# Issuing a step's side tasks between its two score groups in a two-layer attention kernel

## The chip, the cores and the metric

One core of one Trainium2 chip runs the whole kernel. The metric is device time in microseconds; three executions of the kernel before gave 825.37, 826.34 and 826.98 us (median 826.34).

## What is computed

`x` is 8 images of 32 x 32 positions with 128 channels, all float32. Two layers follow each other:

```
layer 0: t   = layernorm(x); q, k, v = t @ w_qkv + b_qkv            (8 heads of 16)
         out = softmax(q k^T / 4) v ;  x = x + out @ w_out + b_out  (1024 queries x 1024 keys per head)
layer 1: tokens = x @ Win + b_in ; t = layernorm(tokens) ; q, k, v = t @ Wq, Wk, Wv
         pk, pv = 4 x 4 means of k and v (64 positions)
         scores of all queries against pk; the 16 positions with the largest maximum are selected
         attention over those 16; tokens += result
         t2 = layernorm(tokens); tokens += gelu(t2 @ Wf1 + bf1) @ Wf2 + bf2
         out = tokens @ Wout + bout
```

## The kernel before

Almost all of the work is the attention of layer 0. For one image it is cut into 32 **steps** (`STEPS`): four pairs of heads (`PAIRS`) times eight blocks of 128 keys (`TILES`). In step s of image n

- TensorE makes the **scores** of both heads for two halves of the queries: `scores(n, s, 0)` and `scores(n, s, 1)` (L611), two matmuls each (L621). They go to the two halves `S[:, 0]` and `S[:, 1]` of one PSUM tensor. The first group waits until the first exponential of the step before has read its half, the second until the second has;
- ScalarE turns each group into probabilities, `exps(n, s, 0)` and `exps(n, s, 1)` (L846, L852): one ACTIVATE over 128 x 1024 each, into one of three buffers `Pr`;
- TensorE makes the **weighted sums** of the values, `weighted(n, s)` (L625, L636), eight matmul records for each step of keys. `sums_behind` (L80) says which are issued in step s. In images 0 and 7, and in the first 13 steps of image 1, it is the step before; everywhere else odd steps have none, and even ones those of the two steps before. Two are left behind step 31;
- VectorE divides a pair's sums (`divide_o`, L1063) once its eight steps are done, and SyncE moves the result into `attnT`.

Everything else is hung into these steps as **tasks**, by fixed tables (`AT_...`, `USUAL`, `ENDING`, L54 to L63): `before_tasks` prepare the next image (normalise and transpose, steps 6 and 10; q in 17 and 19; k in 21 and 23; v in 25 and 29; the bound on the scores in 28 and 30; the token projection in 32 and 37, which are steps 0 and 5 of the image's own attention); `after_tasks` do layer 1 of the image before (projection 3, transposes 12, q 13, pooled keys 15, scores of the selection 18 to 21 (L687), their maximum 22 (L693) and 23, selection 25, attention over the 16 in 27 to 31, and, already in the steps of the image after, the feed-forward part in 33 to 43, which are 1 to 11). So steps 2, 4, 14, 16, 24 and 26 have no TensorE task. Image 7 and what follows it use `ENDING`.

TensorE fills one PSUM bank with a task's result (`A` for `before_tasks`, `BC0` and `BC1` in turn for `after_tasks`), and VectorE or ScalarE empties it; a later task waits until its bank is empty (`a_turn`, `b_turn`) or its input is there (`b_ready` and other waits). Every engine works through its instructions in the order in which the program gives them. ScalarE and VectorE have their own loops over the steps: ScalarE does the two exponentials of a step and then its share of that step's tasks (L920 to L929); VectorE only its tasks, with `divide_o` at the head of steps 8, 16 and 24.

TensorE's loop before is

```
for s in range(STEPS):
    scores(n, s, 0)
    scores(n, s, 1)
    for behind in sums_behind(n, s):
        weighted(n, behind)
    (the tasks of step s)
```

Of the kernel before, what the change touches and what calls it, by code (L numbers as in the profile page):

```python
# [33 lines left out]
TILES = T // P  # L34
# [6 lines left out]
STEPS = PAIRS * TILES  # L41
# [38 lines left out]
def sums_behind(n, s):  # L80

    if n in (0, IMAGES - 1) or (n == 1 and s < LIGHT):
        return (s - 1,) if s > 0 else ()
    return (s - 2, s - 1) if s % 2 == 0 and s > 0 else ()


def xn_steps(n):
# [46 lines left out]
def two_layers(nc, x, ln_scale, ln_bias, w_qkv, b_qkv, w_out, b_out, Win, b_in, Wq, Wk, Wv, g1, be1, g2, be2,  # L134
# [11 lines left out]
    with ExitStack() as ctx:  # L146
# [132 lines left out]
        def wait_for_flag(eng, n):  # L279

            if n == 0:
                eng.wait_ge(first_dve, FIRST_FLAG)
            else:
                eng.wait_ge(a_drained, a_after(n, "flag", 0))
# [254 lines left out]
        def _(pe):  # L539
# [23 lines left out]
            def before_tasks(n, s):  # L563
                if s in xn_steps(n):
                    h = xn_steps(n).index(s)
                    pe.wait_ge(xn_ready, n + 1)
                    a_turn(n, "xn", h)
                    for t in range(4):
                        mm = pe.transpose(A[:, t * P:(t + 1) * P], xn[:, 4 * h + t, :], ident[:, :])
                    mm.then_inc(a_filled, 1)  # L570
                if s in AT_Q + AT_K:
                    c, h = (0, AT_Q.index(s)) if s in AT_Q else (C, AT_K.index(s))
                    a_turn(n, "k" if c else "q", h)
                    pe.matmul(A[:, :], wqkv_s[:, c:c + C], half(xnT, h), start=True, stop=True).then_inc(a_filled, 1)  # L574
                if s in AT_V:
                    a_turn(n, "v", AT_V.index(s))
                    by_token(A, a_filled, [(xnT, wqkv_s[:, 2 * C:3 * C])], AT_V.index(s))
                if s in AT_TOKX:
                    a_turn(n, "tokx", AT_TOKX.index(s))
                    by_token(A, a_filled, [(xhT, win_s[:, :])], AT_TOKX.index(s))  # L580
                if s == AT_BOUND:
                    pe.wait_ge(squares_ready, n)
                    a_turn(n, "bound", 0)
                    sums_of_squares(A, a_filled)
                if s == AT_FLAG:
                    a_turn(n, "flag", 0)
                    pe.transpose(A[0:1, 0:P], peak[:, :], ident[:, :]).then_inc(a_filled, 1)

            def row_maxima(n):

                for j in range(PAIRS):
                    pe.wait_ge(stack_in[j], 32 + 16 * STACK_DMAS * (n + 1))
                if n > 0:
                    pe.wait_ge(probs_ready, 2 * STEPS * n)
                pe.sem_inc(pe_passed, 1)
                with pe.Fori(0, TILES) as t:
                    pe.wait_ge(tile_copied, TILES * n + t + 1)
                    for h in range(HEADS):
                        pe.wait_ge(max_drained, MAX_TILES * n + HEADS * t + h + 1)
                        r = 64 * (h % 2)  # L600
                        for c in range(2):
                            mm = pe.matmul(S[:, h % 2, c * HALF:(c + 1) * HALF], Qt[r:r + MROW, h // 2, :],
                                           Ks[r:r + MROW, h // 2, c * HALF:(c + 1) * HALF], start=True, stop=True)
                        mm.then_inc(max_filled, 1)
                pe.wait_ge(max_drained, 2 + MAX_TILES * (n + 1))
                pe.sem_inc(pe_passed, 1)
                pe.transpose(S[0:MAX_TILES, 0, 0:P], mx[:, :], ident[:, :]).then_inc(max_turned, 1)
                pe.wait_ge(mneg_ready, n + 1)
                pe.wait_ge(mrow_in, 16 * HEADS * (n + 1))

            def scores(n, s, c):  # L611

                j, kb = s // TILES, s % TILES
                before = 2 * STEPS * n + 2 * s + c - 1
                if before > 0:
                    pe.wait_ge(probs_ready, before)
                if kb == 0 and c == 0:
                    pe.wait_ge(stack_in[j], 32 + 16 * STACK_DMAS * (n + 1))
                for a in range(2):
                    head = slice(64 * a, 64 * a + MROW + 1)  # L620
                    mm = pe.matmul(S[:, c, a * HALF:(a + 1) * HALF], Ks[head, j, kb * P:(kb + 1) * P],  # L621
                                   Qs[head, j, c * HALF:(c + 1) * HALF], start=True, stop=True)
                mm.then_inc(scores_ready, 1)

            def weighted(n, s):  # L625

                j, kb = s // TILES, s % TILES
                pe.wait_ge(probs_ready, 2 * STEPS * n + 2 * s + 2)
                if kb == 0:
                    pe.wait_ge(va_ready, PAIRS * n + j + 1)  # L630
                    if n > 0 or j > 0:
                        pe.wait_ge(o_turned, PAIRS * n + j)
                for a in range(2):
                    for c in range(2):
                        r = 32 * (2 * a + c)
                        mm = pe.matmul(O[r:r + 32, :], Va[:, kb, 2 * j + a, :], Pr[:, (STEPS * n + s) % 3, c, a * HALF:(a + 1) * HALF],  # L636
                                       start=(kb == 0), stop=(kb == TILES - 1))
                mm.then_inc(pv_done, 1)
# [161 lines left out]
            def image(n):  # L800

                wait_for_flag(pe, n)
                pe.sem_inc(pe_passed, 1)
                with pe.If(pe.value_load(flag[0:1, 0:1], min_val=0, max_val=HEADS) > 0):
                    row_maxima(n)
                with pe.Else():
                    pe.sem_inc(max_filled, MAX_TILES)
                    pe.sem_inc(max_turned, 1)
                for s in range(STEPS):
                    scores(n, s, 0)  # L810
                    scores(n, s, 1)
                    for behind in sums_behind(n, s):
                        weighted(n, behind)
                    if n > 0:
                        before_tasks(n, STEPS + s)
                    if n + 1 < IMAGES:
                        before_tasks(n + 1, s)
                    if n > 1:
                        after_tasks(n - 2, STEPS + s)
                    if n > 0:  # L820
                        after_tasks(n - 1, s)
                for behind in sums_behind(n, STEPS):
                    weighted(n, behind)

            image(0)

            pe.wait_ge(weights_in, 16 * WEIGHT_DMAS)
            pe.wait_ge(first_dve, FIRST_DVE)
            for n in range(1, IMAGES):
                image(n)  # L830
# [499 lines left out]
```

## Time and profile before

| | |
|---|---|
| median of three executions | 826.34 us |
| the profiled execution | 827.2 us, its span 825.5 us |
| TensorE busy | 778.4 us (94%) |
| ScalarE busy | 604.1 us (73%) |
| VectorE busy | 506.5 us (61%) |
| GpSimd busy | 164.5 us (20%) |
| TensorE clock, mean over the span | 0.983 of full speed |

The times in the rows are microseconds from the start of the span. PE is TensorE, ACT ScalarE, DVE VectorE, POOL GpSimd. Busy time of an engine is the union of its instructions, so that overlapping matmuls count once and a short wait inside a merged group doesn't show as idle. Images 2 to 6 repeat every 92.2 us; image 3 begins at 278.3, image 7 at 647.2.

### The profile page before, as it was taken

Reading aid. Unit: us, or ns where it says so; the run is one execution under the profiler, and the core shown is the slowest. Engines: PE = TensorE matmul, PEld = TensorE weight load, DVE = VectorE, ACT = ScalarE, POOL = GpSimd, SP = SyncE. Lnnn points to the kernel's source line nnn. Section 1 sums busy time; section 2 is a strip of 40 time slices with the busy share of each in tenths; the row PEclk is TensorE's granted clock in tenths of the full one; section 3 lists DMA queues with packets and bytes.
Section 4 is the critical chain, followed back from the end, with each engine's and each line's share of the span. In section 5 each row is a group of like instructions: output and inputs, shape, how many; then the busy total and the mean of one; then the engine's idle time right before and its main releaser. Section 6 shows DMA issues by size and latency. Waiting matters only on the chain.

```text
span 825.5 us, 14363 instructions
## 1 busy us (share of the span) xinstructions
PE 778.4 (94%) x5079; PEld 373.3 (45%) x5079; DVE 506.5 (61%) x1518; ACT 604.1 (73%) x683; POOL 164.5 (20%) x198
## 2 busy tenths in 40 slices
PE   8889899999999999999999999999999989899987
PEld 6322343355534544355534554354534444245555
DVE  6415446777567865777567865777367753367465
ACT  4697789778887788778878788778878677574112
POOL 2620523221241032121141033112011011000100
PEclk9999999999999999999999999999999999699979
DMA  3553343333243252333253253324153232200400
GB/s 73 95 91 70 66 73 76 72 65 59 58 115 53 47 97 56 81 59 64 54 119 53 45 96 71 73 51 72 21 122 55 48 62 54 55 8 7 103 0 26
DMA packets 45308, 52.89 MB, mean 64 GB/s; under 512 B 15920, under 2 KB 33968, under 8 KB 45232
## 3 DMA queue, kind: packets, MB, share of 16 engines
q1 hardware_dynamic: 45232, 51.92, 32.5%
q8 instruction: 42, 0.69, 0.4%
q14 instruction: 34, 0.28, 0.1%
HBM read 5.45 MB, written 4.19 MB: 12 GB/s over the span
## 4 chain that ended last, share of the span: by engine, by line
PE 62%; ACT 15%; issue 6%; DVE 5%; ACTq 0%; DVEq 0%
PE O L636 21%; PE S L621 15%; ACT Pr L852 10%; PE BC L650 6%; PE BC L642 3%; PE BC L687 3%; PE BC L733 2%; PE BC L747 2%; PE BC L669 2%; PE A L650 2%; PE A L574 2%; PE S L836 1%; ACT hT L892 1%; ACT L852 1%; ACT L892 1%
## 5 line engine op out<-in xcount | busy, mean ns | idle before, releaser
L852 ACT ACTIVATE Pr<-S 128x1024 f32<-128x1024 f32 x512 | 491.5, 1029 | 123.5 <-PE S L621 119.8
L636 PE MATMUL O<-Pr,Va 128*32 128x512 f32 x2048 | 256.7, 606 | 1.8 <-DVE OT L1069 1.1
L621 PE MATMUL S<-Qs,Ks 49*128 49x512 f32 x1024 | 217.3, 471 | 24.6 <-ACT Pr L852 22.0
L621 PEld LDWEIGHTS S<-Qs,Ks 49*128 49x128 f32 x1024 | 87.6, 185 | 172.3 <-ACT Pr L852 135.0
L636 PEld LDWEIGHTS O<-Pr,Va 128*32 128x32 f32 x2048 | 50.0, 109 | 104.6 <-issue 96.9
L501 POOL TENSOR_TENSOR q1l<-q1T,q1h 128x1024 fp32r<-128x1024 f32 x8 | 19.1, 2389 | 217.5 <-DVE q1h L1119 217.5
L1143 DVE TENSOR_REDUCE r<-BC 128x1 f32<-128x512 f32 x64 | 41.4, 685 | 32.7 <-PE BC L687 32.5
L1069 DVE STREAM_TRANSPOSE OT<-O 128x512 f32<-128x512 f32 x32 | 22.8, 713 | 52.1 <-PE O L636 51.9
L462 POOL TENSOR_SCALAR xn<-X,ln 128x128 f32<-128x128 f32 x56 | 45.8, 830 | 3.7 <-DVE ln L982 3.7
L493 POOL TENSOR_TENSOR squares<-qh 128x1024 bf16<-128x1024 f32 x7 | 13.3, 1893 | 151.2 <-DVE hot L1165 112.4
L515 POOL TENSOR_TENSOR tokx<-tokx_new,tok_bias 128x1024 f32<-128x1024 f32 x8 | 19.0, 2370 | 120.1 <-DVE tokx_new L988 120.1
L867 ACT ACTIVATE tT<-BC,cols 128x512 f32<-128x512 f32 x32 | 23.4, 778 | 24.1 <-PE BC L642 24.1
L1210 DVE TENSOR_SCALAR hT<-BC,cols 128x512 f32<-128x512 f32 x32 | 24.0, 751 | 26.5 <-PE BC L733 25.0
L484 POOL TENSOR_SCALAR tokx_new<-win_sum,ln 128x128 f32<-128x128 f32 x64 | 37.4, 605 | 1.4 <-POOL tokx L515 1.3
L1215 DVE TENSOR_TENSOR Y<-BC,out_bias 128x512 f32<-128x512 f32 x16 | 11.0, 690 | 42.9 <-PE BC L747 42.9
L473 POOL COPY Va<-v_new 128x256 f32<-128x256 f32 x32 | 11.8, 399 | 112.9 <-PE O L636 95.5
L687 PE MATMUL BC<-Q1s,K1s 96*128 96x512 f32 x64 | 31.0, 561 | 3.1 <-issue 2.4
L733 PE MATMUL BC<-tT,wf_s 128*128 128x512 f32 x64 | 31.7, 616 | 1.1 <-ACT tT L867 0.5
L747 PE MATMUL BC<-w2o,hT 128*128 128x128 f32 x256 | 32.1, 280 | 0.0
L747 PEld LDWEIGHTS BC<-w2o,hT 128*128 128x128 f32 x256 | 29.6, 192 | 4.7 <-issue 4.7
L574 PE MATMUL A<-xnT,wqkv_s 128*128 128x512 f32 x56 | 31.5, 645 | 0.0
L886 ACT ACTIVATE E<-E 128x512 f32<-128x512 f32 x16 | 9.4, 632 | 26.8 <-DVE E L1182 26.7
(189 smaller groups left out, 989.6 us busy)
## 6 DMA issues: line engine op xcount, KB each, us to landing
Qs<-qh SPq DMA_DIRECT2D x128, 64.0 KB, 2.3
Ks<-kh SPq DMA_DIRECT2D x128, 64.0 KB, 2.3
Q1s<-q1h SPq DMA_DIRECT2D x64, 128.0 KB, 2.4
X<-in_x_dram SPq DMA_DIRECT2D x8, 512.0 KB, 4.2
Qs<-ql SPq DMA_DIRECT2D x64, 64.0 KB, 2.4
Ks<-kl SPq DMA_DIRECT2D x64, 64.0 KB, 2.3
attnT<-On SPq DMA_DIRECT2D x128, 32.0 KB, 2.0
Q1s<-q1l SPq DMA_DIRECT2D x32, 128.0 KB, 2.4
```

What stands on the lines that cost most here:

```text
L462: ins = pool.tensor_scalar(xn[:, t, :], X[:, t, :], ln[:, 0, t:t + 1], ln[:, 1, t:t + 1], ALU.subtract, ALU.mult)
L484: ins = pool.tensor_scalar(tokx_new[:, t, :], win_sum[:, :], ln0[n % 2][:, 0, t:t + 1], None, ALU.mult)
L574: pe.matmul(A[:, :], wqkv_s[:, c:c + C], half(xnT, h), start=True, stop=True).then_inc(a_filled, 1)
L621: mm = pe.matmul(S[:, c, a * HALF:(a + 1) * HALF], Ks[head, j, kb * P:(kb + 1) * P], Qs[head, j, c * HALF:(c + 1) * HALF], start=True, sto ...
L636: mm = pe.matmul(O[r:r + 32, :], Va[:, kb, 2 * j + a, :], Pr[:, (STEPS * n + s) % 3, c, a * HALF:(a + 1) * HALF], start=(kb == 0), stop=(k ...
L642: mm = pe.transpose(bank[:, t * P:(t + 1) * P], src[:, 4 * h + t, :], ident[:, :])
L650: mm = pe.matmul(bank[:, t * P:(t + 1) * P], lhs[:, c:c + P], w, start=(i == 0), stop=(i == len(pairs) - 1))
L687: pe.matmul(bank[:, :], K1s[:, j, :, :].rearrange("p a b -> p (a b)"), half(Q1s[0:ROWS1, j, :], h), start=True, stop=True).then_inc(filled, 1)
L733: pe.matmul(bank[:, :], wf1_s[:, f * C:(f + 1) * C], half(tT, h), start=True, stop=True)\
L747: mm = pe.matmul(BC[h][:, t * P:(t + 1) * P], hT[:, f, c:c + P], w2o[:, f, :], start=False, stop=(t == 3 and f == 1))
L852: act.activation(Pr[:, g % 3, c, :], S[:, c, :], ACT.Exp, scale=SCALE).then_inc(probs_ready, 1)
L1143: ins = dve.tensor_reduce(r8[:, 2 * j + h:2 * j + h + 1], bank[:, :], AX.X, ALU.max)
```

## The change

In every step but the first of each pair of heads (steps 0, 8, 16 and 24), TensorE issues the tasks of the step behind the first score group, ahead of the second. No instruction is added or taken away, and the loops of the other engines stay as they are.

```diff
@@ -82,6 +82,11 @@
+def tasks_between(n, s):
+
+    return s % TILES > 0
@@ -806,11 +811,7 @@
-                for s in range(STEPS):
-                    scores(n, s, 0)
-                    scores(n, s, 1)
-                    for behind in sums_behind(n, s):
-                        weighted(n, behind)
+                def tasks(s):
                     if n > 0:
                         before_tasks(n, STEPS + s)
                     if n + 1 < IMAGES:
...
                     if n > 0:
                         after_tasks(n - 1, s)
+
+                for s in range(STEPS):
+                    scores(n, s, 0)
+                    if tasks_between(n, s):
+                        tasks(s)
+                    scores(n, s, 1)
+                    for behind in sums_behind(n, s):
+                        weighted(n, behind)
+                    if not tasks_between(n, s):
+                        tasks(s)
                 for behind in sums_behind(n, STEPS):
                     weighted(n, behind)
```

Two places of TensorE's order. The first is from the tasks of step 21 to that of step 22 in image 2. Of before (L621 scores, L636 weighted sums, L574 the next image's k, L687 the selection's scores, L693 the transpose of their maximum `r1`; `b_drained` and `c_drained` say that `BC0` and `BC1` have been read):

```order
L574 MATMUL A<-xnT,wqkv_s 128x512 [waits a_drained]
L687 MATMUL BC0<-Q1s,K1s 128x512 [waits b_drained]
L687 MATMUL BC1<-Q1s,K1s 128x512 [waits c_drained]
L621 MATMUL S<-Qs,Ks 128x512 [waits probs_ready]
L621 MATMUL S<-Qs,Ks 128x512
L621 MATMUL S<-Qs,Ks 128x512 [waits probs_ready]
L621 MATMUL S<-Qs,Ks 128x512
L636 MATMUL O<-Pr,Va 32x512 [waits probs_ready]
L636 MATMUL O<-Pr,Va 32x512 x3
L636 MATMUL O<-Pr,Va 32x512 [waits probs_ready]
L636 MATMUL O<-Pr,Va 32x512 x3
L693 MATMUL BC0<-ident,r1 1x128 [waits c_drained,b_drained]
```

and of the change (its lines stand five further down: L579, L692, L626, L698, L641):

```order
L579 MATMUL A<-xnT,wqkv_s 128x512 [waits a_drained]
L692 MATMUL BC0<-Q1s,K1s 128x512 [waits b_drained]
L692 MATMUL BC1<-Q1s,K1s 128x512 [waits c_drained]
L626 MATMUL S<-Qs,Ks 128x512 [waits probs_ready]
L626 MATMUL S<-Qs,Ks 128x512
L626 MATMUL S<-Qs,Ks 128x512 [waits probs_ready]
L626 MATMUL S<-Qs,Ks 128x512
L698 MATMUL BC0<-ident,r1 1x128 [waits c_drained,b_drained]
L626 MATMUL S<-Qs,Ks 128x512 [waits probs_ready]
L626 MATMUL S<-Qs,Ks 128x512
L641 MATMUL O<-Pr,Va 32x512 [waits probs_ready]
```

In the second listing the first two pairs of L626 are the second group of step 21 and the first of step 22. Between the selection's scores and the transpose there were two score groups and two weighted sums; now there are two score groups, and the second group of step 22 and the sums stand behind the transpose.

The second place is from step 29 to step 30 of the same image. Before:

```order
L650 MATMUL A<-wqkv_s,xnT 128x128 x3
L621 MATMUL S<-Qs,Ks 128x512 [waits probs_ready]
L621 MATMUL S<-Qs,Ks 128x512
L621 MATMUL S<-Qs,Ks 128x512 [waits probs_ready]
L621 MATMUL S<-Qs,Ks 128x512
L636 MATMUL O<-Pr,Va 32x512 [waits probs_ready]
L636 MATMUL O<-Pr,Va 32x512 x3
L636 MATMUL O<-Pr,Va 32x512 [waits probs_ready]
L636 MATMUL O<-Pr,Va 32x512 x3
L587 MATMUL A<-ident,peak 1x128 [waits a_drained]
L642 MATMUL BC0<-ident,E2 128x128 [waits b_drained,e2_ready]
```

and of the change:

```order
L655 MATMUL A<-wqkv_s,xnT 128x128 x3
L626 MATMUL S<-Qs,Ks 128x512 [waits probs_ready]
L626 MATMUL S<-Qs,Ks 128x512
L626 MATMUL S<-Qs,Ks 128x512 [waits probs_ready]
L626 MATMUL S<-Qs,Ks 128x512
L592 MATMUL A<-ident,peak 1x128 [waits a_drained]
L647 MATMUL BC0<-ident,E2 128x128 [waits b_drained,e2_ready]
```

The transposes of step 30 (the bound's `peak`, and the small attention's `E2`) follow v's projection of step 29 with two score groups between them, and without the two weighted sums.

## Rows read from the trace of the kernel before

**Rows 1.** The page: busy time, the clock by slices, the chain that ended last.
```profile
PE 778.4 (94%) x5079; PEld 373.3 (45%) x5079; DVE 506.5 (61%) x1518; ACT 604.1 (73%) x683; POOL 164.5 (20%) x198
...
PEclk9999999999999999999999999999999999699979
...
PE 62%; ACT 15%; issue 6%; DVE 5%; ACTq 0%; DVEq 0%
```

**Rows 2.** Groups of instructions: count, busy us, mean ns, idle time before and releasers.
```profile
L852 ACT ACTIVATE Pr<-S 128x1024 f32<-128x1024 f32 x512 | 491.5, 1029 | 123.5 <-PE S L621 119.8 <-issue 2.4
...
L621 PE MATMUL S<-Qs,Ks 49*128 49x512 f32 x1024 | 217.3, 471 | 24.6 <-ACT Pr L852 22.0 <-issue 0.7 <-DMA Ks<-kh 0.5
```

**Rows 3.** L621 alone in image 3: stretch, PE busy, PEld busy, clock, DMA.
```profile
278.30:370.50 92.20, 26.60 (x128) 10.77 (x128) 1.00 0.36 70
```

**Rows 4.** Windows of images 0 and 3: busy PE, PEld, DVE, ACT, POOL; clock.
```profile
27.30:102.50 75.20, 66.93 (x423) 20.58 (x423) 26.81 (x89) 62.91 (x68) 24.86 (x31) 1.00 0.44 80
...
278.30:370.50 92.20, 89.94 (x606) 42.89 (x602) 62.39 (x188) 74.67 (x84) 21.44 (x24) 1.00 0.36 70
```

**Rows 5.** Timeline, first two steps of image 0: start, us, what [idle before].
```profile
27.33 0.73 PE L621 MATMUL S<-Qs,Ks 49*128 49x512 f32 x4 [0.51 <-DMA Ks<-kh]
27.88 2.86 ACT L852 ACTIVATE Pr<-S 128x1024 f32<-128x1024 f32 x3 [6.31 <-PE S L621]
28.95 0.50 PE L621 MATMUL S<-Qs,Ks 49*128 49x512 f32 x2 [0.89 <-ACT Pr L852]
```

**Rows 6.** Timeline of PE, steps 20 to 22 of image 3.
```profile
339.41 0.73 PE L687 MATMUL BC<-Q1s,K1s 96*128 96x512 f32 x2
340.07 0.73 PE L621 MATMUL S<-Qs,Ks 49*128 49x512 f32 x4
...
341.30 1.03 PE L687 MATMUL BC<-Q1s,K1s 96*128 96x512 f32 x2
342.26 0.85 PE L621 MATMUL S<-Qs,Ks 49*128 49x512 f32 x4
343.05 1.92 PE L636 MATMUL O<-Pr,Va 128*32 128x512 f32 x16
344.98 0.27 PE L693 MATMUL BC<-ident,r 128*1 128x128 f32 x1
```

**Rows 7.** Timeline of DVE over the same steps.
```profile
341.90 0.75 DVE L995 TENSOR_SCALAR kh<-A,cols 128x512 fp32r<-128x512 f32 x1 [0.67 <-PE A L574]
...
343.36 1.28 DVE L1143 TENSOR_REDUCE r<-BC 128x1 f32<-128x512 f32 x2
344.67 0.16 DVE L1148 TENSOR_REDUCE r<-r 128x1 f32<-128x8 f32 x1
```

**Rows 8.** Timeline, steps 28 to 30 of image 3.
```profile
359.83 1.15 ACT L886 ACTIVATE E<-E 128x512 f32<-128x512 f32 x2
...
364.33 0.68 DVE L1000 TENSOR_TENSOR v_new<-A,rows 128x512 f32<-128x512 f32 x1
...
365.15 0.27 PE L587 MATMUL A<-ident,peak 128*1 128x128 f32 x1
```

**Rows 9.** Timeline, image 7: from the copy of layer 1's q to step 17's task.
```profile
694.52 0.69 DVE L1119 CAST q1h<-q1T 128x1024 fp32r<-128x1024 f32 x1 [2.19 <-ACT q1T L873]
...
704.62 1.19 PE L687 MATMUL BC<-Q1s,K1s 96*128 96x512 f32 x2 [1.79 <-issue]
```

**Rows 10.** Timeline, steps 7 to 9 of image 3.
```profile
297.44 4.02 PE L733 MATMUL BC<-tT,wf_s 128*128 128x512 f32 x8
...
304.90 2.86 ACT L852 ACTIVATE Pr<-S 128x1024 f32<-128x1024 f32 x3
...
305.98 0.50 PE L621 MATMUL S<-Qs,Ks 49*128 49x512 f32 x2
```

**Rows 11.** Image 7: the step after, and the window (columns as in Rows 4).
```profile
708.76 1.22 PE L687 MATMUL BC<-Q1s,K1s 96*128 96x512 f32 x2
...
704.00:717.70 13.70, 13.08 (x44) 4.12 (x44) 3.87 (x6) 5.81 (x6) 0.00 (x0) 0.50 0.17 49
```

## The prediction

> **What bounds the kernel now.** I read the page first. TensorE is busy 94% of the span and the chain that ended last is 62% TensorE's, 15% ScalarE's [rows 1]. ScalarE waits 119.8 us for scores; TensorE waits 22.0 us in the open for exponentials [rows 2]. More waits hide inside merged groups: one step's four score matmuls take 0.73 us where nothing holds them [rows 5, 6], so 256 steps need 187 us, and the groups are busy for 217.3 [rows 2]. The windows then show where: in image 3, which stands for images 2 to 6, the scores are busy 26.6 us against 32 x 0.73 = 23.4 [rows 3], so all that TensorE loses there to late exponentials is about 3.2 us of 92.2, at full clock [rows 4]. That is the most this change can win in such an image: it moves work and removes none. ScalarE is busy 74.7 of the 92.2 us, with 17 us to spare. The kernel is bound by TensorE's own work in a closely packed order, and the question is what the new order makes it wait for.
>
> **Units, from the timelines.** Two score groups are busy 0.73 us and two weighted sums 1.92 [rows 6]; each overlaps its neighbour by 0.06, so I count 0.67 and 1.86, and 0.33 or 0.34 for one group. Behind a group that had to wait the sums start 0.43 after it: from S1 over two sums to the next S0 are 2.3. An exponential starts 0.55 after its score group and takes 1.03 [rows 2, 5], and the group that reuses its half starts 0.05 later: 27.33 to 28.95, **1.62 us from a score group to the same group of the next step** [rows 5]. With T(s) for the tasks of step s, an even and the next odd step now read S0 T S1 sums | S0 T S1.
>
> **a. The second exponential loses its cover.** Before, between S1 of an odd step and S1 of the even step behind it stood T(odd) and S0. Now stand there S0 and T(even). T(odd) is often 1 to 3 us, but T(even) is often nothing, or, in steps 8, 16 and 24, left at its old place. Then TensorE has 0.34 + 0.34 = 0.68 us of work for a latency of 1.62 and waits 0.94. That is so at steps 2, 4, 14, 16, 24 and 26: 6 x 0.94 = 5.6 us (step 8 is under c). Steps 6 and 10 have four short transposes, +0.57: 2 x 0.37 = 0.7. Step 28 has +0.30: 0.6. Behind step 31 the last weighted sum needs the exponential of a group just issued: 1.62 less 1.29 = 0.3. Behind even steps the sums cover the latency, and the odd steps' tasks cost nothing. Sum of a: **7.3 us** an image.
>
> **b. Tasks of even steps come before their inputs.** The distance from T(odd) to T(even) was two score groups and two sums; the sums, 1.86 us, are gone from it, and what waits now has S1, the sums, and so ScalarE behind it.
> - Step 22, the transpose of `r1`. VectorE starts k's drain 0.60 after the start of the two L687 matmuls (341.30 to 341.90), needs 1.46 for it and 1.28 and 0.16 for the maxima, and the transpose starts at 344.98: 3.68 after 341.30 [rows 6, 7]. TensorE will be there after 0.96 (341.30 to 342.26) and two groups, 0.67: 1.63. It waits **2.05**.
> - Step 20, the same pattern with q's drain: the first bank is free 341.90 + 1.46 + 0.69 - 341.30 = 2.75 after the start, the second at 3.34. TensorE comes at 1.63: 1.1 + 0.3 = **1.4**.
> - Step 30: the transpose of `peak` needs bank A, which v fills in step 29 and VectorE empties only behind the small softmax; from ScalarE's L886 to that transpose it is 5.3 us (359.83 to 365.15) [rows 8]. In the new order L886 starts 1.6 behind S1(28), so the transpose is due at 6.9, or 6.4 if VectorE is free 0.4 earlier, as `peak`'s reduction now comes ahead of S1. TensorE comes at 2.3 + 0.33 + 1.09 + 0.34 + 0.33 = 4.4. It waits 2.0 to 2.5: **2.1**.
> - Step 18 waits for the stacked q of layer 1, which in image 7 came 10.1 us after the copy to `q1h` began [rows 9]; in the other images it came in time, so that is an upper bound elsewhere. The copy follows ScalarE's drain, which now follows the second exponential of step 13: it begins 4.7 behind T(13), and the stack is due at 14.8. Adding the units and the waits of a, TensorE comes at 13.5. It waits **1.2** (0 if the moves are quicker).
> Sum of b: **6.8 us**. Other even steps (12) have inputs two steps old and wait for nothing; odd ones have the sums ahead of them.
>
> **c. The gelu block.** ScalarE loads a table, does two gelus and loads the exponential's table again, and only then does E0(8) at 304.90, which lets S0(9) start at 305.98 [rows 10]. The block used to start behind E1(7), which was early. Now E1(7) waits for T(7), eight matmuls of 3.95 us from S0(7) on. T(7) starts 0.33 earlier, at 297.11, S1(7) at 301.06, E1(7) ends at 302.6, the same 4.6 us follow, and S0(9) comes at 308.3: **+2.3 us**, S1(8)'s own wait inside it.
>
> Against 16.4 stand the 3.2 us of old waits, which go: **+13.1 us for each of images 2 to 6**, 92.2 to about 105. Image 1 has the paired order from step 13 on, where a and b give 12.3 and the old waits 1.8: +10. Image 0 has few tasks, all of the next image's, one sum in every step (0.34 + 0.43 + 0.95 = 1.7, more than the latency), and ScalarE is its bound: the drains no longer wait for the sums; -2. Image 7 has the single sums too, so a falls away; its step 17 waits some 2 us more, pt and tok2 1.7 together, the gelu block 0.7, and about 1.5 of old waits go: +3. Sum 65.5 + 10 - 2 + 3 = **+77 us**. The tail after image 7 is untouched. The change moves no DMA, and neither SyncE's nor GpSimd's queue is passed; both only come later with everything.
>
> **d. The clock.** In image 7, TensorE stood idle for 1.79 us ahead of step 17's task [rows 9], and from 704.0 to 717.7 its granted clock was 0.50, the 1.2 GHz level [rows 11]; before and in the whole of image 3 it was 1.00 [rows 4]. A step there took 4.14 us (704.62 to 708.76) against 0.66 (two L687, 339.41 to 340.07) + 0.67 + 0.95 (one sum and the step over to the next work) = 2.3 for the same at the full clock [rows 6]: 1.8 times. So 13.7 us at the low clock do 7.6 us of work, for which the new order would need 7.6 / 0.87 = 8.7 us with its waits: 5.0 us a fall. The new order makes idle stretches of about 2 us at steps 22 and 30 of images 1 to 6, twelve places. The one like them was followed by a fall, but one case is thin, so I take 8 of 12: **+40 us**; bounds 0 and 60.
> The Trainium skill, "TensorE: Matmul & The Clock Gate", section "A second HAM failure mode: psum-queue depth-cycling", says more: frequent micro-idles between matmul groups are enough to let the clock oscillate. Image 0 speaks against that as it stands: it waits 0.4 to 0.9 us in its steps [rows 5], is busy 66.9 of 75.2 us, and kept clock 1.00 [rows 4]. It is a rival below.
>
> Sum: 827.2 + 77 + 40 = 944, for the profiled execution, which was 0.9 over the median: **943 us**.
>
> **Rivals.**
> - *The waits come, the clock holds.* For it: the waits of image 0 brought no fall, and only one of 1.8 us did. 827 + 77 - 1 = 903.
> - *The waits are half as long*, since VectorE and the moves run ahead once TensorE is slower, and the clock mostly holds: 827 + 39 = 865. Against it: a is bare latency, and b a chain that starts at the task before.
> - *Faster.* The tasks fill the time in which TensorE waits for the second exponential, and ScalarE no longer waits for drains behind the sums. At most 30 us of hidden waits and 22 open ones [rows 2] are there, a third of them in steps without tasks or waits for the first group; half gained: 827 - 20 = 807. The point from which it decides is b's: it needs the inputs of even steps ready within 1.63 us of the task before, where rows 7 give 2.75 and 3.7, and the latency of 1.62 covered by 0.68.
> - *Oscillation throughout.* Images 1 to 6 at the low clock: their work of some 88 us each, times 1.8, is 159, +67 on 92: 827 + 6 x 67 = 1229. By the skill's rule on micro-idles.
> - The order of TensorE's instructions shows that the change does what it says, and all moved waits stand ahead of S1; no change in time would need gain and loss to meet.
>
> **How the numbers follow.** Forecast 943 with several falls: 0.55. Clock holds, 903: 0.26. Half the waits, 865: 0.10. Faster, 807: 0.04. Oscillation: 0.03. Within 0.2% of before, which is what a measurement can tell: 0.02. The range takes the forecast with twelve falls and 0.3 us more in each of b's terms (963 + 7) and the holding clock with step 18 free and b's others 0.2 to 0.5 shorter (903 - 15): 888 to 972. Half waits and the rest stay outside. Slower in all 0.94.
>
> **What would show it.** Images 2 to 6 last 103 to 107 us at full clock, or up to 10 more with falls; second score groups wait about 0.9 us at steps 2, 4, 14, 16, 24, 26; the L698 transpose (old L693) waits 2 us for VectorE, L592 (L587) likewise; S0(9) is 2.3 later from S0(7). The mean clock falls from 0.983 to about 0.9. A period of 92 us or less, or waits for exponentials gone, would prove me wrong; a period of 105 with clock 1.00 picks the first rival.

## The result and the profile after

The changed kernel took 942.89 us (median of 4 executions, 929.94 to 947.45) against 825.86 for the kernel before (4 executions, 822.16 to 826.98): **1.135 times as long, interval 1.129 to 1.140**. This ratio and interval leave out the two longest executions (944.87 and 947.45), which ran at a lower mean clock, 0.951 and 0.949; by the medians over all four it is 1.142. Forecast were 943, between 888 and 972. The profiled execution took 940.92 us, its span 939.2 at a mean clock of 0.956.

The page of the changed kernel: busy time, the clock by slices, the chain that ended last (its lines stand five or eleven further down than before).

```profile
PE 812.8 (87%) x5079; PEld 381.8 (41%) x5079; DVE 504.6 (54%) x1518; ACT 612.9 (65%) x683; POOL 162.5 (17%) x198
...
PEclk8999999999999999999999999999999999669979
...
PE 60%; ACT 12%; DVE 11%; issue 6%; ACTq 0%; DVEq 0%
```

Against [rows 1], the share in which TensorE is busy fell from 94% to 87%, and VectorE's part of the last chain rose from 5% to 11%: TensorE now waits for VectorE. Who waits for whom says it in microseconds. First the changed kernel, TensorE's waits (line, releaser: total, times, longest):

```profile
PE S L626 <- ACT Pr L863: 59.1, 83, 2.1
PE BC L698 <- DVE r L1159: 13.0, 7, 2.0
PE BC L692 <- issue: 12.4, 8, 3.5
PE A L592 <- DVE v_new L1011: 11.8, 6, 2.0
PE BC L692 <- DVE r L1154: 7.5, 9, 1.1
```

The same view of the kernel before has one such row over 3 us, and its wait for `r` is 1.1:

```profile
PE S L621 <- ACT Pr L852: 22.0, 60, 0.9
PE BC L687 <- issue: 2.4, 2, 1.8
...
PE BC L693 <- DVE r L1148: 1.1, 1, 1.1
```

The open waits for exponentials rose by 37 us. The transposes of `r1` (L698, step 22) and of `peak` (L592, step 30) wait 2.0 us at most and 13.0 and 11.8 in all, the layer-1 scores (L692) for free banks (step 20) and for the stacked q (step 18, "issue"; image 7's 3.5 us is one of these) another 20.

The windows of images 0 and 2, columns as in [rows 4]:

```profile
30.71:102.95 72.24, 66.76 (x423) 20.98 (x422) 25.72 (x85) 63.52 (x68) 24.83 (x31) 1.00 0.44 77
202.01:311.39 109.38, 93.38 (x602) 43.46 (x603) 62.34 (x189) 75.67 (x84) 21.08 (x25) 0.98 0.30 59
```

Images 2 to 6 last 108.9 to 109.7 us where they lasted 92.2. TensorE is busy 3.4 us longer in one, and idle 16.0 us where it was 2.3. Image 0 is 2.9 us shorter: 72.24 from its first score to image 1's, before 75.15.

Where the 113.7 us between the two profiled spans went, by the starts of the images:

| | before | after | difference |
|---|---|---|---|
| up to image 0 | 27.3 | 30.7 | +3.4 |
| image 0 | 75.2 | 72.2 | -2.9 |
| image 1 | 83.9 | 99.1 | +15.1 |
| images 2 to 6 | 460.8 | 546.0 | +85.2 |
| image 7 and the tail | 178.3 | 191.2 | +12.9 |

The 3.4 us ahead of image 0 are not the change's, which moves nothing there. In the profiles of all twelve kernels this stretch goes with the clock: image 0 starts at 27.3 where no low clock was granted ahead of it (before, and one kernel below), at 28.1 to 28.8 with 3.4 us at 0.50 (six kernels), at 29.4 and 29.6 with 6.8, and at 30.7 and 30.8 with 10.2 (the change and step 7 alone).

### The profile page after: what moved, and what is told of

It is laid out like the page before. It is cut to its first block, busy times and chain, and to the rows that moved or that the text cites. A ratio compares the mean times of both kernels' runs of the same rounds, so it can differ in the third digit from the quotient of the medians.

```text
span 939.2 us, 14363 instructions
## 1 busy us (share of the span) xinstructions
PE 812.8 (87%) x5079; PEld 381.8 (41%) x5079; DVE 504.6 (54%) x1518; ACT 612.9 (65%) x683; POOL 162.5 (17%) x198
## 4 chain that ended last, share of the span: by engine, by line
PE 60%; ACT 12%; DVE 11%; issue 6%; ACTq 0%; DVEq 0%
PE O L641 19%; PE S L626 14%; ACT Pr L863 9%; PE BC L655 5%; PE BC L738 3%; PE BC L647 3%; PE BC L752 3%; PE A L579 3%; PE A L655 2%; DVE r L1154 2%; PE BC L674 2%; PE BC L692 1%; PE S L847 1%; DVE den L1201 1%; ACT hT L903 1%
## 5 line engine op out<-in xcount | busy, mean ns | idle before, releaser
L863 ACT ACTIVATE Pr<-S 128x1024 f32<-128x1024 f32 x512 | 502.0, 1028 | 252.1 <-PE S L626 248.5
L626 PE MATMUL S<-Qs,Ks 49*128 49x512 f32 x1024 | 233.9, 485 | 62.3 <-ACT Pr L863 59.1
L641 PE MATMUL O<-Pr,Va 128*32 128x512 f32 x2048 | 271.9, 635 | 1.8 <-ACT Pr L863 0.9
L626 PEld LDWEIGHTS S<-Qs,Ks 49*128 49x128 f32 x1024 | 93.1, 188 | 277.5 <-ACT Pr L863 214.3
L641 PEld LDWEIGHTS O<-Pr,Va 128*32 128x32 f32 x2048 | 50.3, 111 | 105.5 <-issue 81.9
L692 PE MATMUL BC<-Q1s,K1s 96*128 96x512 f32 x64 | 31.5, 555 | 20.7 <-issue 12.4
L467 POOL TENSOR_SCALAR xn<-X,ln 128x128 f32<-128x128 f32 x56 | 43.9, 796 | 3.4 <-DVE ln L993 3.4
L478 POOL COPY Va<-v_new 128x256 f32<-128x256 f32 x32 | 11.8, 399 | 151.0 <-DVE v_new L1011 96.7
L1006 DVE TENSOR_SCALAR kh<-A,cols 128x512 fp32r<-128x512 f32 x14 | 10.5, 750 | 45.7 <-PE A L579 45.7
L579 PE MATMUL A<-xnT,wqkv_s 128*128 128x512 f32 x56 | 32.5, 661 | 0.0
```

Source lines behind the costliest of these rows:

```text
L467: ins = pool.tensor_scalar(xn[:, t, :], X[:, t, :], ln[:, 0, t:t + 1], ln[:, 1, t:t + 1], ALU.subtract, ALU.mult)
L692: pe.matmul(bank[:, :], K1s[:, j, :, :].rearrange("p a b -> p (a b)"), half(Q1s[0:ROWS1, j, :], h), start=True, stop=True).then_inc(filled, 1)
L863: act.activation(Pr[:, g % 3, c, :], S[:, c, :], ACT.Exp, scale=SCALE).then_inc(probs_ready, 1)
```

## Three places of the changed kernel

Steps 21 and 22 of image 5, timeline of TensorE and VectorE (start, duration, what, idle before):

```profile
600.17 1.03 PE L692 MATMUL BC<-Q1s,K1s 96*128 96x512 f32 x2
600.77 0.75 DVE L1006 TENSOR_SCALAR kh<-A,cols 128x512 fp32r<-128x512 f32 x1 [3.08 <-PE A L579]
601.13 0.73 PE L626 MATMUL S<-Qs,Ks 49*128 49x512 f32 x4
...
603.54 0.16 DVE L1159 TENSOR_REDUCE r<-r 128x1 f32<-128x8 f32 x1
603.85 0.27 PE L698 MATMUL BC<-ident,r 128*1 128x128 f32 x1 [1.99 <-DVE r L1159]
```

From the start of the two L692 to the transpose it is 603.85 - 600.17 = 3.68 us, to the hundredth what it was in [rows 6, 7]. VectorE did its part at the same pace; only what TensorE had done in the meantime, the two weighted sums, is gone. Forecast were 2.05 us of wait; 1.99 stand open here, and by the starts it is 2.05.

Steps 1 and 2 of image 5, an even step without a task:

```profile
532.16 1.09 PE L647 MATMUL BC<-ident,E 128*128 128x128 f32 x8
533.18 0.75 PE L626 MATMUL S<-Qs,Ks 49*128 49x512 f32 x4
533.72 1.02 ACT L863 ACTIVATE Pr<-S 128x1024 f32<-128x1024 f32 x1 [0.35 <-PE S L626]
534.80 0.50 PE L626 MATMUL S<-Qs,Ks 49*128 49x512 f32 x2 [0.87 <-ACT Pr L863]
```

The row of four matmuls is the second score group of step 1 and the first of step 2. From there to the second group of step 2 it is 1.62 us (533.18 to 534.80), the latency of [rows 5], with 0.68 of work in it.

Step 17 of image 7, and the clock in what follows (columns as in [rows 4]):

```profile
807.68 1.19 PE L692 MATMUL BC<-Q1s,K1s 96*128 96x512 f32 x2 [3.54 <-issue]
```

```profile
807.00:837.70 30.70, 30.02 (x105) 9.06 (x109) 8.18 (x21) 14.22 (x14) 0.00 (x0) 0.50 0.08 22
```

TensorE waits 3.5 us for the stacked q instead of [rows 9]'s 1.8. The clock stands at the 1.2 GHz level from 807.0, 0.7 us before that wait ends, for 30.7 us instead of 13.7 [rows 11].

## The experiments

Each edits the condition `tasks_between` of the changed kernel unless it says otherwise. One line stands for a diff where only that condition differs. Nothing of the computation is left out in any. The first four kernels, the fifth ("without the late inputs") and the first with a sum between ran once each; beside the first four the kernel before took 824.58, also once, and its medians beside the others were 826.03 and 827.85, of 11 executions each that spread over 822 to 831. So small differences are read from the images of the profiles, not from one total.

### The tasks of step 22 alone

```diff
-    return s % TILES > 0
+    return s == 22
```

> The old order, with the tasks of step 22 alone between the two score groups. My account (term b, a task ahead of its input): the transpose of r1 is due 3.7 us after the start of the two L692 matmuls of step 21 and TensorE comes after 1.3, so it waits 2.4 us in each of images 1 to 6: 14 us, plus some 5 us if the clock falls at several of them: 841 to 850 us. Rival (VectorE runs ahead once TensorE is slower, half the wait): 833. Rival (the loss of the change is mostly the clock, not the waits): under 835 with clock 0.98.

847.87 us, 23 more than before. Image 3 of this kernel:

```profile
353.31 0.27 PE L698 MATMUL BC<-ident,r 128*1 128x128 f32 x1 [2.21 <-DVE r L1159]
...
354.10 3.39 PE L641 MATMUL O<-Pr,Va 128*32 128x512 f32 x16
357.42 0.73 PE L626 MATMUL S<-Qs,Ks 49*128 49x512 f32 x4
```

The total lies in the expected range (841 to 850). One moved transpose makes TensorE idle for 2.2 us, and the two weighted sums behind it, 1.92 us before [rows 6], take 3.39: the clock has fallen. It fell in each of images 1 to 6, each time in or just behind this step, for 3.4 us. The images last 95.6 to 95.9 us, +3.6. In the sum of images 1 to 6, 22 us. The wait and the fall that it brings are both shown, on one edit.

### The tasks of step 7 alone

```diff
-    return s % TILES > 0
+    return s == 7
```

> The old order, with the tasks of step 7 alone between the two score groups. My account (term c): the gelu block starts behind E1(7), which now waits for the eight matmuls; S0(9) comes 2.4 us later in images 2 to 6 and 0.7 in image 7: 839 to 841 us. Rival (ScalarE's slack of 17 us an image takes it up): 827.

845.22 us. Two images of it:

```profile
189.86:284.20 94.34, 90.38 (x607) 42.91 (x604) 62.66 (x189) 74.81 (x84) 21.48 (x24) 1.00 0.35 68
284.20:380.09 95.89, 91.98 (x606) 44.32 (x603) 62.62 (x189) 74.81 (x84) 21.49 (x24) 0.98 0.35 67
```

Image 2 kept its clock and is 2.1 us longer than before, as expected to 0.3. Image 3 had one fall of 3.4 us (2 us behind the wait of step 9) and is another **1.55 us** longer: the price of a fall. Three of the five images 2 to 6 had one, and are 1.5, 2.1 and 1.5 us longer than image 2. The total is 4 us over the expected range, by these falls and by a start that was late by as much as in the changed kernel.

### Even steps alone, odd steps alone

```diff
-    return s % TILES > 0
+    return s % TILES > 0 and s % 2 == 0     (even steps)
+    return s % 2 == 1                       (odd steps)
```

> Tasks between in even steps that are no multiple of 8, the old place in odd ones. Term b without a and c: waits of about 1.6 (step 6, bank A), 2.1 (18), 1.7 (20), 2.4 (22) and 2.6 (30) against 1.1 of old waits that go: +9.5 us for each of images 2 to 6 (period 101 to 102), 8 in image 1, some 3 in image 7: 885 to 890 us, and up to 15 more through falls of the clock. Rival (term a is the loss, b small): 835.

> Tasks between in odd steps, the old place in even ones. Terms a and c without b: 14 even steps lose the cover of the second exponential, 0.94 each, +0.3 at the end and +2.4 for the gelu block, less 3.2 of old waits: +12.7 us for each of images 2 to 6 (period about 105), 9 in image 1: 895 to 905 us at nearly the clock of before, as no idle stretch is longer than 1.3 us. Rival (b and the clock are the loss): 840.

Even steps 916.39 us, odd steps 915.62, both over their expectations (at most 905). An image of the first and one of the second:

```profile
523.61:629.69 106.08, 95.98 (x607) 44.33 (x603) 62.90 (x189) 75.50 (x84) 21.27 (x24) 0.95 0.31 61
```

```profile
300.95:408.31 107.36, 91.67 (x603) 43.00 (x603) 62.23 (x189) 75.50 (x84) 21.10 (x25) 1.00 0.31 60
```

Each half of the change alone costs over three quarters of the whole, by different means. With even steps the tasks wait for inputs (by the starts, in images 1 to 6: 2.4 us at step 22, 1.4 to 2.3 at 6, 1.8 to 3.4 at 18, 2.1 at 30, 1.5 at 20; 2.4, 1.6, 2.1, 2.6 and 1.7 were expected), and the clock fell 20 times in images 1 to 6. At 1.55 each that is 31 us where up to 15 were expected, and 5 us of image 5's 13.9 over before; without them its period is the expected 101 to 102. With odd steps the clock of images 1 to 6 stayed at 1.00 throughout; every even step but the first waits 0.94 us for its second exponential, and the period is 107.4 where I expected 105. Its 15.1 us over before are terms a and c alone, and 2.4 of them had no name yet.

### Without the late inputs

```diff
-    return s % TILES > 0
+    return s % TILES > 0 and s not in (18, 20, 22, 30)
```

> The change, but the tasks of steps 18, 20, 22 and 30 stay at their old place. Their waits for inputs (1.0 to 1.9, 1.4, 2.0 and 2.0 us) become the 0.94 us of an uncovered second exponential: 3 us an image less than the change, and without idle stretches of 2 us no falls of the clock in images 1 to 6, another 1.5 us each: a period of 104 to 106 us instead of 109, 910 to 920 us in all. Rival (the falls come from the many waits of 0.9 us, not from the long ones): the clock of those images still falls.

904.01 us. The clock didn't fall once in images 1 to 6:

```profile
297.38:401.87 104.49, 91.54 (x603) 43.00 (x603) 62.28 (x189) 75.25 (x84) 21.15 (x25) 1.00 0.32 62
```

Four of the 32 steps' places carry 4.7 us of the 17 an image: 3.1 by waits and 1.55 by the fall. The many waits of 0.9 us bring no fall. The expectation for the total was 6 us too high: against the changed kernel, image 7 and the tail are 4.2 us shorter and the start 3.4, and the expectation counted neither.

### The first weighted sum between the score groups

The changed loop, with the older of an even step's two sums between the groups; in the first kernel together with the tasks, in the second with the tasks at their old place, in the third, in the images with paired sums, with those of steps 1, 9 and 15:

```diff
+def halves(behind):
+    return (behind[:1], behind[1:]) if len(behind) == 2 else ((), behind)
...
                     scores(n, s, 0)
+                    between, behind_all = halves(sums_behind(n, s))
+                    for behind in between:
+                        weighted(n, behind)
                     if tasks_between(n, s):
                         tasks(s)
                     scores(n, s, 1)
-                    for behind in sums_behind(n, s):
+                    for behind in behind_all:
                         weighted(n, behind)
```

> The change, and in addition the first of an even step's two weighted sums ahead of its tasks, between the score groups; it needs nothing that isn't long ready. If a is bare latency, the sum's 0.93 us cover it (0.34 + 0.34 + 0.93 = 1.61 of 1.62), and b's four waits get shorter by 0.93 each, while c stays: 7.3 + 3.7 us an image less than the change, a period of 98 to 99 us, 870 to 885 us in all. Rival (TensorE's switches between kinds of matmul cost it, or the waits are of another kind): 930 or more.

> Tasks at their old place; only the first of an even step's two weighted sums goes between the score groups. The old waits for the second exponential in even steps (0.26 + 0.08 + 0.47 + 0.22 + 0.38 = 1.4 us an image) go, nothing new is waited for: 818 to 820 us. Rival (the later second group delays ScalarE, which is then late for the next step): 826 or more.

> As the kernel before it, and the tasks of steps 1, 9 and 15 between as well, whose inputs are early and whose next even step now has the sum as cover: another 0.44 + 0.57 + 0.18 = 1.2 us an image: 812 to 814 us. Rival (moving tasks ahead of a second group always costs the cover): 0.9 us lost at each of the three, 830 or more.

The first: 899.26 us, where 870 to 885 were expected; an image without a fall lasts 101.8 us, where 98 to 99 were expected. The wait of 0.94 is gone from every even step, so it was latency that lacked cover; but 3 us an image stay. The second says what they are: 834.40 us, ratio 1.011 (1.007 to 1.014), a little **slower** than before where I expected a gain. Image 3 of it:

```profile
286.27:380.10 93.83, 93.05 (x607) 41.99 (x603) 62.79 (x189) 75.91 (x84) 21.28 (x24) 1.00 0.35 69
```

It is idle for 0.8 us only, against 2.3 before, but busy for 3.1 us more with the same matmuls [rows 4]. Step 8 of image 3 before, a pair of groups and a pair of sums, and step 2 of this kernel's image 3:

```profile
301.39 0.73 PE L621 MATMUL S<-Qs,Ks 49*128 49x512 f32 x4
302.06 1.92 PE L636 MATMUL O<-Pr,Va 128*32 128x512 f32 x16
303.91 2.05 PE L740 MATMUL BC<-wout_s,Y 128*128 128x128 f32 x16
```

```profile
290.25 0.49 PE L631 MATMUL S<-Qs,Ks 49*128 49x512 f32 x2
...
290.67 1.06 PE L646 MATMUL O<-Pr,Va 128*32 128x512 f32 x8
...
291.67 0.49 PE L631 MATMUL S<-Qs,Ks 49*128 49x512 f32 x2
292.09 1.06 PE L646 MATMUL O<-Pr,Va 128*32 128x512 f32 x8
293.09 0.86 PE L631 MATMUL S<-Qs,Ks 49*128 49x512 f32 x4
```

From start to start, the pair of groups takes 0.67 and the pair of sums 1.85, 2.52 together; alone, a group takes 0.42 and a sum 1.00, and the four make 2.84. **A score group or a sum that stands alone between other kinds of matmul costs some 0.08 us more than half a pair**, so an even step with two further changes of kind costs 0.33 more, 0.16 a change. Steps 4, 10, 16 and 28, which had nothing to wait for before, are longer by just that (0.32 to 0.35) in each of images 2 to 6. Fifteen even steps would be 4.9 us; the waits that go give back all but 1.6 of it. (The 3.1 us of busy time are less, since some of the old waits were hidden in busy rows.)

It is also a part of the nameless 2.4 us of the odd steps. A group that had to wait takes 0.42 as well, and in image 3 of that kernel 30 of the 64 groups take 0.42 or 0.43, against 13 before: 1.5 us. Another 0.5 stand ahead of each next image's first scores, and the old waits were larger than 3.2 (below), which goes the other way. What else is in it wasn't taken apart.

The third, 833.28 us, ratio 1.009 (1.006 to 1.012), was expected at 812 to 814. It gains 0.4 us between steps 9 and 11, loses 0.4 between steps 1 and 4, and has nothing from step 15; the two kernels can't be told apart.

### What was good in the change

In the first image, and wherever each step has one weighted sum, the new order had saved time. The next kernel keeps only that; the last adds step 9, and the sum between in three steps where more than 0.2 us are to be had:

```diff
+    if n == 0:
+        return s % TILES > 0
+    if n == 1:
+        return 0 < s < LIGHT and s % TILES > 0
+    if n == IMAGES - 1:
+        return s in (1, 3, 5, 9, 11)
+    return False                     (the last kernel: s == 9, and halves only in steps 10, 18 and 30)
```

> Tasks between only where each step has one weighted sum (image 0, image 1 up to step 12, and steps 1, 3, 5, 9 and 11 of image 7). In the profile of the change image 0 is 2.9 us shorter, image 1 gains 0.5 to 0.9 up to there, and image 7 some 2 in these steps: 5 to 6 us less than before, 819 to 821 us. Rival (the gain is lost to what comes behind): 825 or more.

> As the kernel before it, and in the paired images the tasks of step 9 between, with the first sum between in steps 10, 18 and 30: 0.35 + 0.25 + 0.16 us an image by the profiles of the two kernels that had them, after the 0.2 us that each further switch costs: another 4 us, 815 to 817 us. Rival (these small gains don't add): as the kernel before it, 820.

818.70 us, ratio **0.990 (0.986 to 0.994)**, and 816.85 us, **0.988 (0.984 to 0.992)**. Both beat the kernel before and the changed one. They can't be told from each other by these intervals. Part of either gain is the clock, whose mean was 0.988 and 0.986 in their executions and 0.983 in those of before. Executions at 0.990 alone have spans of 815.3 to 817.0 (the first), 813.3 (the last, one) and 821.0 and 821.9 (before): 5 us and some 8 are the new order's, and 5 to 6 were expected of the first. Image 0 of the first, and image 3 of the second:

```profile
28.64:100.88 72.24, 66.73 (x422) 20.95 (x422) 26.49 (x89) 63.51 (x68) 24.86 (x31) 1.00 0.46 83
```

```profile
277.01:368.81 91.80, 90.44 (x606) 42.54 (x602) 62.70 (x189) 74.92 (x84) 21.49 (x24) 1.00 0.36 70
```

The image 0 is that of the changed kernel to the hundredth. The paired images of the last last 91.2 to 91.8 us, those of the one before it 91.8 to 92.6. Of the 0.6 us between them steps 9 and 10 give 0.35 and step 18 0.15; step 30 gives nothing.

## Why the prediction was right, and where its terms were off

The total was met to a tenth of a microsecond, but that is luck: its terms erred in opposite directions by 11 and 14 us, and the four executions themselves lie 17.5 us apart. What held is the mechanism. Point by point:

- **a, the second exponential loses its cover.** Right in mechanism and size. The wait at each empty even step is 1.62 - 0.68 = 0.94, as the timeline shows; putting a sum there removes it. Behind step 31 the last sum waits the 0.3 that were forecast, but the next image's first scores come 0.5 later again.
- **b, tasks before their inputs.** Right at steps 22 (2.05 forecast, 2.05 by the starts), 20 (1.4 against 1.5) and 30 (2.1 against 2.0). Step 18 was forecast at 1.2 and waited 1.0 to 1.9, differently by image; what makes the difference stays open.
- **c, the gelu block.** Forecast +2.3 from S0(7) to S0(9); the change gave 2.4, step 7 alone 2.1 on the image.
- **The waits' sum was too small: 77 us, where some 88 came.** "I count 0.67 and 1.86, and 0.33 or 0.34 for one group" is the term that was off: it priced a lone group like half a pair. In image 3 of the change 31 of the 64 groups take 0.42 or 0.43, before 13; without a fall an image would be 107.6 and not 105, outside the 103 to 107 given as a sign. A second reading partly hid this: the old waits were taken as 3.2 us from busy time, in which an open wait doesn't show, and they count as the most that the change could win. From start to start, image 3's groups before take 26.5 us where 32 x 0.67 = 21.4 would do: 5.1, of which 1.2 are groups at 0.42. Image 1 had the same (+15.1 with two falls, against +10), and **image 7** was forecast at +3 and took 13.9 to its end. In it 37.5 us were at the low level instead of 13.7, at 0.47 for each an estimated 11 us, most of it around its 3.5 us wait.
- **d, the clock, was too dear: 40 us, where about 26 came.** The number of falls was near, 7 in images 1 to 6 of 8 forecast, but not their places: of the twelve stretches at steps 22 and 30 five were followed by a fall, and the other two falls came behind step 18 and step 20. I took the length from one fall, 13.7 us in image 7 (the tail has another of that length, at 782.6), and a price of 5.0; these lasted 3.4 us and cost 1.55 [image pair of step 7 alone]: 11 us. The rest is image 7 and the tail, 48 us at the low level instead of 27, and the start with 10 instead of none. The executions give the same price from outside: the two in the ratio had mean clocks of 0.968 and 0.956 and spans of 928.2 and 939.2, so 11.0 us more span go with some 23 us more at the half clock, 0.48 for each; the other two (0.951 and 943.1, 0.949 and 945.7) lie on the same line, 0.47 over all four. From the kernel before, 27 us at low clock, to this execution, 82, that is 26 us. The other 88 are waits and lone groups. The mean clock was 0.956 and not the "about 0.9" given as a sign.
- **The rivals.** "The waits come, the clock holds" (903) fell: the clock fell in each of images 1 to 6, and and the waits alone would have given some 827 + 88 = 915, not 903. That the kernel without the late inputs took 904 is no support for it, since its waits are 3.1 us an image less. "Half the waits" fell: they came whole. "Oscillation throughout" fell too. It was named after the Trainium skill, "TensorE: Matmul & The Clock Gate", section "A second HAM failure mode: psum-queue depth-cycling", by which frequent micro-idles let the clock oscillate; here odd steps alone have 15 waits of some 0.9 us in each of images 2 to 6, and not one fall there. "Faster" was right in one place, the images with one sum a step, -2.9 us in image 0 against -2 forecast.
- A slip without weight: the upper end of the range, 972, is 2 over the sum given for it (963 + 7).

Why one order gains in image 0 and loses in image 3, as far as it is argued from these lengths and not tried apart: with one sum in every step, a sum stands behind each second score group, 1.7 us of work against 1.62 of latency, and the tasks in front cost it nothing, while ScalarE's drains no longer wait for the sum. With sums paired into even steps, an odd step's second group has nothing behind it.

## What to carry to other kernels

In a loop where two engines hand a double buffer back and forth, write down for each buffer half how much work stands between its fill and its next fill, and compare it with the round trip (here 1.62 us); work moved to hide one wait uncovers the neighbour's. An in-order queue gives a task's input exactly the time of what stands between, so the price of moving a task forward is the age of its input, which the trace tells to the hundredth. And of interleaving, count what it leaves standing alone: a split pair of score groups and a split pair of sums cost 0.33 us a step here, 4.9 us an image, and the waits that this filled were 3.3.

## What the runs showed of the hardware that was not expected

- A score group (49 rows by 128 columns) alone between other kinds of matmul takes 0.42 to 0.43 us from start to start, in an unheld pair 0.33 to 0.34; a weighted sum (128 by 32) alone takes 1.00, in a pair 0.93. A group that had to wait takes 0.42 too.
- One idle stretch of 2.2 us of TensorE was followed by a fall to the half clock in six images of six (step 22 alone). Stretches of 2.0 us in the change were followed by one in five of twelve; stretches of 1.3 us ahead of step 9 in three of five with step 7 alone, but in none of five with the odd steps, where nearly the same stretch stands. What else decides it stays open. Waits of 0.9 us, 15 in each of images 2 to 6 with the odd steps, never brought one there.
- A fall doesn't have one length: 3.4 us behind the waits of images 1 to 6 (1.5 to 2.1 us lost), 13.7 us in image 7 of before, 30.7 us around the wait of 3.5 us in the change. Nor does the wait alone give it: in image 1 of the even steps a wait of 3.2 us was followed by a fall of 3.4. Why some of image 7's are longer wasn't tried.
